# Layer two of a mixture of experts: VectorE transposes dense blocks, TensorE's combination reads with a step, and its products go to four row strips at a time

## The reference: what is computed

```python
grouped = x.reshape(B, g, t, d)                       # 32 groups of t = 32 tokens per sequence
logits = jnp.einsum('bgtd,des->bgtes', grouped, controller) + tie
perm = (logits == jnp.max(logits, axis=-3, keepdims=True)).astype(x.dtype)
dispatched = jnp.einsum('bgtd,bgtes->bgesd', grouped, perm)
inner = jax.nn.relu(jnp.einsum('bgesd,desf->bgesf', dispatched, f1) + bias)
intermediate = jnp.einsum('bgesf,esfd->bgesd', inner, f2)
out = jnp.einsum('bgesd,bgtes->bgtd', intermediate, perm)
```

## Time and profile before

| | before |
|---|---|
| median of 3 runs | 1348.98 us (1346.82 to 1352.07) |
| profiled execution: time | 1353.44 us |
| profiled execution: span from the first to the last instruction | 1351.7 us |
| PE busy | 1203.2 us (89%) |
| DVE busy | 890.0 us (66%) |
| ACT busy | 612.6 us (45%) |
| POOL busy | 583.6 us (43%) |
| mean granted TensorE clock | 0.930 of full |

### The profile page before, as it was taken

The page is one execution under the profiler, slowest core; times in us unless marked ns, Lnnn a source line. Parts: engine busy times, 40 slices in busy tenths (PEclk is TensorE's granted clock), DMA queues, the critical chain, the costliest instruction groups (busy, mean ns, idle before and its releaser), DMA issues. The chain is left out here.

```text
span 1351.7 us, 29427 instructions
## 1 busy us (share of the span) xinstructions
PE 1203.2 (89%) x11456; PEld 830.9 (61%) x11456; DVE 890.0 (66%) x2198; ACT 612.6 (45%) x1143; POOL 583.6 (43%) x799
## 2 busy tenths in 40 slices
PE   5999999976889999999999999993799988898773
PEld 4888888853445555555555555541588877875552
DVE  6555555525666877777777778740578865559994
ACT  3222222201545555556656566552244444366651
POOL 0000000003446767777666666674576734302333
PEclk9999999995999999999999999997799977678986
DMA  6665555549623455555554444203788955453344
GB/s 228 217 217 207 213 210 209 186 156 198 143 68 77 108 126 126 126 126 126 126 125 106 114 113 113 69 17 112 266 260 264 297 168 188 168 190 89 111 128 148
DMA packets 163885, 210.77 MB, mean 156 GB/s; under 512 B 8880, under 2 KB 96560, under 8 KB 162736
## 3 DMA queue, kind: packets, MB, share of 16 engines
q1 hardware_dynamic: 163760, 209.06, 53.3%
HBM read 131.17 MB, written 77.59 MB: 154 GB/s over the span
## 5 line engine op out<-in xcount | busy, mean ns | idle before, releaser
L718 ACT ACTIVATE p_t<-p_bank 128x512 f32<-128x512 f32 (+1 forms) x608 | 310.2, 589 | 222.9 <-PE p_bank L778 217.3
L759 PE MATMUL p_bank<-k_stack,q_stack 96*128 96x512 f32 (+3 forms) x768 | 285.2, 394 | 28.8 <-DMA ident<-in_ident 19.3
L664 DVE CUSTOM_DVE_ANT_0 tried<-p_bank,ban 128x128 bf16<-128x128 f32 (+3 forms) x512 | 236.5, 485 | 86.1 <-PE p_bank L759 86.0
L778 PE MATMUL p_bank<-q_stack,k_stack 97*128 97x512 f32 (+3 forms) x768 | 258.9, 358 | 10.4 <-ACT p_t L718 6.0
L759 PEld LDWEIGHTS p_bank<-k_stack,q_stack 96*128 96x128 f32 x768 | 145.8, 193 | 152.8 <-issue 64.2
L667 DVE TENSOR_REDUCE mx_a<-p_bank 128x1 f32<-128x512 f32 x256 | 175.9, 687 | 62.5 <-PE p_bank L759 61.0
L600 POOL TENSOR_SCALAR_AFFINE_SELECT p_t<-p_t 128x128 f32<-128x128 f32 (+2 forms) x288 | 102.0, 357 | 171.5 <-ACT p_t L718 164.2
L778 PEld LDWEIGHTS p_bank<-q_stack,k_stack 97*128 97x128 f32 x768 | 145.6, 191 | 41.5 <-ACT p_t L718 27.0
L796 PE MATMUL p_bank<-p_t,v_tile 128*32 128x512 f32 (+3 forms) x1536 | 162.9, 497 | 1.6 <-POOL p_t L600 1.2
L611 POOL TENSOR_TENSOR p_sum<-p_sum,p_t 128x512 f32<-128x512 f32 x128 | 159.9, 1281 | 0.5 <-ACT p_t L718 0.5
L584 POOL MEMSET k_stack<- 1x4096 f32 x3 | 10.4, 3506 | 302.3 <-POOLq L128 302.3
(11 more groups left out here) (121 smaller groups left out, 2287.8 us busy)
## 6 DMA issues: line engine op xcount, KB each, us to landing
q_stack<-q_hi SPq DMA_DIRECT2D x64, 256.0 KB, 6.5
k_stack<-k_hi SPq DMA_DIRECT2D x30, 512.0 KB, 9.5
f_sb<-in_f SPq DMA_DIRECT2D x5, 2048.0 KB, 7.9
x_in<-in_x SPq DMA_DIRECT2D x8, 1024.0 KB, 9.1
c_in<-in_ctx_t SPq DMA_DIRECT2D x8, 1024.0 KB, 11.1
k_hi<-k_hi_s SPq DMA_DIRECT2D x8, 1024.0 KB, 4.2
k_lo<-k_lo_s SPq DMA_DIRECT2D x8, 1024.0 KB, 6.4
v_rows<-v_out SPq DMA_DIRECT2D x8, 1024.0 KB, 4.3
```

The source lines that it names most:

```text
L664: dve.tensor_tensor_reduce(tried[:, TRIED[c]:TRIED[c] + w], got, ban0[:] if i == 0 else ban[:, CH - w:CH], 1.0, -3e38, ALU.add, ALU.max, t ...
L718: act.activation(pt[:, k % SLOTS_P, u * m:(u + 1) * m, 0:w], bank[:, SB + n % SR, 0:m * w].rearrange("p (m w) -> p m w", m=m), ACT.Exp, sc ...
L759: pe.matmul(bank[:, to, 0:w], qs[it % SLOTS][0:R, i * P // CH, h, i * P % CH:i * P % CH + P], ks[it % SLOTS][0:R, h, t0:t0 + w], start=Tru ...
L778: mm = pe.matmul(bank[:, SB + n % SR, h % m * w:(h % m + 1) * w], ks[slot][0:R + 1, h, j * P:(j + 1) * P], qs[slot][0:R + 1, sh, h, CH - w ...
```

## The change

`y` is laid out the other way round: `[d, i]` (feature, then expert within the strip) instead of `[i, d]`, and so are the two `y_rows`: `[d, g]` instead of `[g, d]`. VectorE's transpositions then read and write 1024 elements that lie one behind another, where they read with a step of 256 elements (1024 bytes) and wrote with a step of 128 elements (512 bytes). TensorE's combine now reads its 128 moving columns out of `y_rows` with a step of 32 elements (128 bytes), where they were contiguous. ScalarE's keep now takes its elements from PSUM with the bank as the innermost index and writes runs of 4 elements (16 bytes) every 128 bytes, where it read and wrote contiguous runs.

A make now covers two pairs. Which expert sits in which strip and place is permuted (in layer one, and on the host in `f2` and the bias) so that those two pairs use all four row strips `q` with all four column strips `c`: the same 32 products, now with 16 different positions of the array before the first is used again, where a pair used 8. It waits for the banks of both pairs before its first product, and it releases both at its last ones. The makes of unit `u + 2` are split into two pairs after chunk 0 and six after chunk 1.

```diff
-        y = [wide[:, i * IDX * DH:(i + 1) * IDX * DH].rearrange("p (i d) -> p i d", d=DH) for i in range(2)]
-        y_rows = [nc.alloc_sbuf_tensor_at(f"y_rows{i}", [P, GT, P], F32, offset=at)
+        y = [wide[:, i * IDX * DH:(i + 1) * IDX * DH].rearrange("p (d i) -> p d i", i=IDX) for i in range(2)]
+        y_rows = [nc.alloc_sbuf_tensor_at(f"y_rows{i}", [P, P, GT], F32, offset=at)
...
-                    to = y[u % 2].rearrange("p (m q) d -> p q m d", q=4)[:, qp * 2:qp * 2 + 2, mp * 2:mp * 2 + 2]
-                    act.copy(to, bank[:, n % RING * 2:n % RING * 2 + 2].rearrange("p q (m d) -> p q m d", m=2)).then_inc(kept_y, 1)
+                    to = y[u % 2][:, :, pair * 4:pair * 4 + 4].rearrange("p d (m q) -> p d m q", q=2)
+                    act.copy(to, bank[:, n % RING * 2:n % RING * 2 + 2].rearrange("p q (m d) -> p d m q", m=2)).then_inc(kept_y, 1)
...
-                            for pair in (range(RING) if ch == 0 else range(RING, PAIRS)):
+                            for pair in (range(2) if ch == 0 else range(2, PAIRS)):
                                 keep(u + 2, pair)
...
-                        ins = dve.transpose(y_rows[ch][:, :, d:d + ONCE].rearrange("p g d -> p d g"),
-                                            y[u % 2][:, :, ch * P + d:ch * P + d + ONCE].rearrange("p i d -> p d i"))
+                        ins = dve.transpose(y_rows[ch][:, d:d + ONCE],
+                                            y[u % 2][:, ch * P + d:ch * P + d + ONCE])
...
-                                es = e * IDX + n * 4 + q
+                                es = e * IDX + n // 2 * 8 + q // 2 * 4 + n % 2 * 2 + q % 2
...
-                def make(u, pair):
-
-                    b, h, mp, qp = u // HALVES, u % HALVES, pair // 2, pair % 2
-                    n = u * PAIRS + pair
+                def make(u, mp):
+
+                    b, h = u // HALVES, u % HALVES
                     if u == 0:
                         pe.wait_ge(f2_in[mp], 16)
                         pe.wait_ge(active, mp * 2 + 2)
-                    if n >= RING:
-                        pe.wait_ge(kept_y, n - RING + 1)
-                    else:
-                        pe.wait_ge(inner_done, (KD - 1) * NQ + n * 2 + 2)
+                    for n in (u * PAIRS + mp * 2, u * PAIRS + mp * 2 + 1):
+                        if n >= RING:
+                            pe.wait_ge(kept_y, n - RING + 1)
+                        else:
+                            pe.wait_ge(inner_done, (KD - 1) * NQ + n * 2 + 2)
                     for i in range(2):
-                        for q in range(qp * 2, qp * 2 + 2):
-                            part = slice(q * F, (q + 1) * F)
-                            for c in range(4):
+                        for c in range(4):
+                            for q in range(4):
+                                part = slice(q * F, (q + 1) * F)
                                 e = (mp * 2 + i) * 4 + c
+                                n = u * PAIRS + mp * 2 + q // 2
                                 mm = pe.matmul(bank[c * GT:(c + 1) * GT, n % RING * 2 + q % 2, i * DH:(i + 1) * DH],
                                                inner[part, e, b * GT:(b + 1) * GT], f2[e // PIECE][part, e % PIECE, h * DH:(h + 1) * DH],
                                                start=True, stop=True, tile_position=(q * F, c * GT), skip_group_check=True)
-                    mm.then_inc(made, 1)
+                                if i == 1 and c == 3 and q % 2 == 1:
+                                    mm.then_inc(made, 1)
...
-                                               pick[:, i, g * GT:(g + 1) * GT], y_rows[ch][:, (w * UT + n) * GQ + g],
+                                               pick[:, i, g * GT:(g + 1) * GT], y_rows[ch][:, :, (w * UT + n) * GQ + g],
...
-                            for pair in (range(RING) if ch == 0 else range(RING, PAIRS)):
-                                make(u + 2, pair)
+                            for mp in (range(1) if ch == 0 else range(1, PAIRS // 2)):
+                                make(u + 2, mp)
```

More of the change, by code:

```diff
@@ L1481, in _ @@
                 for u in range(2):
-                    for pair in range(PAIRS):
-                        make(u, pair)
+                    for mp in range(PAIRS // 2):
+                        make(u, mp)
                 for u in range(UNITS):
@@ L1541, in layout @@
         "f1": arr(i["L0_ffn_f1"]).reshape(D, NE * F),
-        "bias_col": arr(arr(i["L0_ffn_bias"]).reshape(4, E4 // 4, 4, F).transpose(2, 3, 1, 0)).reshape(P, E4),
-        "f2": arr(arr(i["L0_ffn_f2"]).reshape(4, E4 // 4, 4, F, D).transpose(2, 3, 1, 0, 4)).reshape(P, E4, D),
+        "bias_col": arr(arr(i["L0_ffn_bias"]).reshape(4, 4, 2, 2, 2, F).transpose(2, 4, 5, 1, 3, 0)).reshape(P, E4),
+        "f2": arr(arr(i["L0_ffn_f2"]).reshape(4, 4, 2, 2, 2, F, D).transpose(2, 4, 5, 1, 3, 0, 6)).reshape(P, E4, D),
         "ident": np.eye(P, dtype=np.float32),
```

## The result

The changed kernel takes 1374.34 us (median of 4 runs, 1372.32 to 1378.62), the kernel before, run beside it, 1350.53 us (4 runs, 1346.82 to 1356.97). The ratio is 1.0161, with a 95% interval from 1.0128 to 1.0193: 1.6% slower. The forecast was 1350, its range 1343 to 1361. The time is near the 1370 of the rival that stepped reads make TensorE the limit.

What follows compares the result with a forecast made beforehand. SyncE's queue of stores and loads was taken as the limit, VectorE close beside it. -2.5 (third store) + 1.4 (start) + 2.1 (clock) = +1.0 us on the median 1348.98 gave 1350.0 us, range 1343 to 1361.

Steps and rivals of the forecast that it cites:

- the rival that stepped reads make TensorE the limit: Combine: stepped reads slow TensorE past the queue; at s = 3 a unit is 18.3 us, time 1370; chance 0.10.
- The limit before: SyncE's queue: 32 sums stored, landed and loaded one by one, 3.88 us each, bound the kernel; VectorE offered one each 3.71.
- The rival that VectorE was the limit: Transpositions: VectorE bound the kernel after all, so 30 us less, 1319 us; chance 0.03.
- VectorE's transpositions: Dense transpositions on VectorE: 1238 ns each instead of 1983, 47.7 us less work over 64.
- The combine's reads: TensorE's stepped reads in the combine: taken to cost 0, upper bound a factor 1.6 from VectorE's rows.
- s = 2.3: Combine: the slowdown factor s at which a unit on TensorE reaches the queue's 15.5 us.
- The makes: TensorE's makes: 1.10 us for two pairs, 2.3 us a round with copy and hand-overs; hidden in the loop, not at the start.
- my formula: TensorE's time for one unit of the loop: 6.6 + 3.9 s us, s being the factor on the combines.
- The start and the clock: Before the first store: slower rounds of makes and copies cost +1.4 us, a lower TensorE clock +2.1 us.
- The clock's term: Makes at the start: a less busy TensorE gets a lower clock, +2.1 us, bounds 0 and +6.2.
- The sum: Whole kernel: -2.5 + 1.4 + 2.1 = +1.0 us, likeliest time 1350.0 us.
- The -2.5 us at the third store: Queue's third store: chunks 4.6 us apart instead of 7.4 end its wait for a sum, saving 2.5 us.

Runs made afterwards that it cites:

- e4: The kernel before with each load one store later in the queue: 1342.81 us, ratio 0.9932.
- e7: The changed kernel with each load one store later in the queue: 1371.87 us, ratio 1.0160.
- e3: The kernel before with only the new makes (permuted experts, two pairs a make, split two and six): 1354.81 us, ratio 0.9999.
- e1: The changed kernel with y_rows back at [g, d], so the combine reads contiguously and VectorE writes with a step: 1353.93 us, ratio 1.0018.
- e8: The kernel before with the combine reading at a step of 32 elements, all four column strips reading the same columns: 1366.64 us in one profiled run.
- e11: The changed kernel with the makes of before (one pair a make, three and five pairs): 1353.79 us, ratio 1.0018.
- e2: The kernel before with only the combine's reads changed, to a step of 32 elements: 1371.36 us, ratio 1.0127.
- e9: The kernel before with y as [d, i], y_rows in runs of two elements, and each load one store later: 1321.04 us, ratio 0.9782.
- e6: The kernel before with y_rows in runs of two elements and each load one store later: 1347.29 us, ratio 0.9968.
- e5: The kernel before with y_rows in runs of four elements and each load one store later: 1349.89 us, ratio 0.9992.

## Why the prediction was wrong

**The limit before: right.** I took the queue, not VectorE, for the limit. e4 moved the loads away from their stores and won 0.7%, and e7 shows that the same edit is worth nothing once TensorE is the limit. Its pace I took for steadier than it is: measured alike, from the first store to the last four, it was 4.26 us a sum before, 4.11 in e3 and 3.86 in e1. And I set a unit at 15.5 us, by the pace of the end, where the same rows give 16.9 for the middle. The rival that VectorE was the limit is out: its row fell by 45 us and the time rose.

**VectorE's transpositions: right.** I said 1238 ns each, and they take 1212; 47.7 us less, and it is 44.9. e1 adds that the whole of it hangs on both sides: with one side stepped by 512 bytes next to nothing is won.

**The combine's reads: the step that failed.** "I take 0", with 1.6 as the upper bound from VectorE's rows. A chunk takes 5.53 to 5.59 us in the chain and 5.65 in the timeline of PE, where it took 1.95, so s is 2.8 to 2.9 at full clock, above the point s = 2.3 that I had named as decisive. With it the overlap on which the forecast stood is gone: I had TensorE at 10.5 us a unit, hidden under the queue's 15.5, and it takes 19.2 to 20.2. The bound was borrowed from another engine, and nothing ties the two. A dense transposition takes 1024 elements a partition in 1212 ns, a dense chunk's combine, counted by its records, 64 x 128 = 8192 columns in 1.95 us, five times as many in a ns. That a limit on reads with a step shows sooner on the faster reader is an argument that no run tests; e8 took one explanation from it, the four separate streams. But it should have kept me from taking VectorE's factor for an upper bound. The rule that I quoted, the Trainium skill's "SBUF — State Buffer", section "SBUF: two separate sides" (at least two hits in each 16-byte line), pointed the right way, and the runs agree with it where they can: a step of 8 bytes, two hits a line, took 1.97 to 2.05 us, one of 16 bytes 3.78 to 3.85. That 128 bytes costs still more, 5.5 to 5.7, the rule does not say.

**The makes: right in kind, too small.** I wrote 1.10 us for two pairs and 2.3 for a round; it is 1.47 and 2.65. The old makes take 0.78 and 0.86 us a pair when they stand back to back (three in 2.35 and five in 4.30 us of e11's chain), 1.57 to 1.72 for two, so sixteen positions save 0.1 to 0.3 us in two pairs, not the 0.5 to 0.6 that 1.10 would have been. The copy at 1.02 and the two hand-overs at 0.16 together were close to what I said (1.1 and 0.1). On a unit this is the smaller part: of the 8.7 us above my 10.5, the combines are 7.2 and the makes with their copies 1.5. By my formula a unit is 6.6 + 3.9 x 2.85 = 17.7 us, whereas the trace has 19.24, and four makes of 1.41 to 1.49 instead of 1.1 are 1.4 of the 1.5 between them. But it is the part that tells, since 17.7 is what e11 has, and e11 is not measurably slower than before. In the first two units of the loop one make ran at half the clock besides, 2.37 us instead of 1.49 (at 1244.29 and 1264.46 us); they took 20.2 us.

**The start and the clock: right in kind, too small.** The first store was to move by 1.4 + 2.1 us and moved by 8.0 from the first copy. Seven rounds of 2.65 instead of 2.3 are 2.5 of that. ScalarE then waits 0.98 us for the first sum, which comes after half a stepped combine; I had it wait for nothing. The clock's term is 3.2 us where I had 2.1 (bounds 0 and 6.2): the seven makes of these rounds take 13.5 us, where seven of 1.47 are 10.3, and 2.7 of the difference lies in the last three, at 2.35 to 2.37 us each. Together 1.4 + 2.5 + 1.0 + 3.2 = 8.1. Two stretches of the start of the changed kernel (busy time of PE, PEld, DVE, ACT and POOL, then granted clock, DMA share, GB/s): TensorE was busy for 6.4 of the first 10 us at the full 2.4 GHz, and in the second, with those three makes, it had 1.2.

```profile
1206.00:1216.00 10.00, 6.41 (x256) 3.51 (x255) 0.79 (x1) 6.59 (x8) 0.00 (x0) 1.00 0.02 7
1217.00:1226.50 9.50, 7.13 (x196) 3.35 (x200) 7.34 (x7) 4.69 (x6) 0.00 (x0) 0.50 0.01 3
```

The stepped combines do not follow the clock. In e2 the first one had it at half for at least 3 of its 5.5 us (the combine in the timeline of PE, then the stretch):

```profile
1225.48 5.54 PE L1472 MATMUL p_bank<-y_rows,pick_exp 128*32 128x128 f32 x64 [1.78 <-DVE y_rows L1389]
...
1226.00:1229.00 3.00, 3.00 (x41) 2.16 (x36) 3.00 (x2) 0.53 (x1) 0.00 (x0) 0.51 0.00 0
```

It takes 5.54 us, and e2's others at full clock 5.57 to 5.66, where a dense one went from 1.95 to 3.62. That would fit a combine that waits for its reads; no run shows what it waits for.

**The sum.** I had 1350 as the likeliest; for it to fail two things had to come together, and both did. Either half of the change alone stays at the queue's pace or close to it (the new makes in e1 and e3, the layout in e11: ratios within 0.2% of 1, their intervals within 0.5%); both together are 19.2 to 20.2 us a unit against 16.9. The -2.5 us at the third store had nothing to act on, since the sums came later and not sooner. My rival for this side had the right limit, TensorE, but gave the reads alone as the cause; it put 18.3 us on a unit at s = 3, against 19.2. That its 20 us on the whole came so near to the 19.4 is partly luck: it was 2.8 us in each of seven units over a queue at 15.5, and nothing at the start, where the trace has 13.5 us in the loop, over a queue at 17.1 a unit (119.4 / 7), and 8.0 at the start. I had given it 0.10.

## What stays open

Why the queue takes 4.26 us a sum in the kernel before and 3.86 in e1 is not settled, and so it is open how far the makes of e1 and e3 would stay hidden at the slower pace. That VectorE's stepped transpositions grow while TensorE reads with a step is measured in e2; which resource the two share was not tried. The new makes bring three things at once, the order of the positions, the wait for two pairs of banks and a lower granted clock, and no run parts them. A ring of more than three pairs of banks, which could keep the new makes from alternating with the copies, was not tried.

## What to carry to other kernels

In these runs an access with a step was cheap or dear by its distance in bytes and by the engine that made it: before a layout is turned for one engine, price the same bytes on the engine on the other side, and look for one that serves both (here runs of two elements with the old makes, 2.2% faster, where the fully dense layout with the new makes lost 1.6%; both with the later loads, which alone gave 0.7%). When two limits lie side by side, two changes that cost nothing alone can cost together, so add their parts on each engine for one round of the loop and not over the whole. A make that must find two of the ring's three buffers empty turned the pipeline into an alternation; count copy plus hand-over plus make as one round.

## What was not expected of the hardware

- Combine of one chunk, 64 records of 128 moving fp32 columns, at full clock: contiguous 1.95 us, step of 8 bytes 1.97 to 2.05, 16 bytes 3.78 to 3.85, 128 bytes 5.5 to 5.7. The last is the same with the clock at half for most of it (e2, 5.54) and when all four column strips read the same columns (e8).
- A 32 x 32 block transposition of 1024 fp32 elements a partition on VectorE: 1212 to 1214 ns when the reading side is dense and the writing side is dense or in runs of 8 or 16 bytes; 1.82 us from one to the next when the writing side alone is stepped by 512 bytes (e1), 1.90 and 1.94 when the reading side alone is, with runs of 8 and 16 bytes written (e6, e5), 1.86 when both are.
- Stepped reads of TensorE slow other engines: with a step of 128 bytes, VectorE's stepped transpositions went from 118.8 to 142.5 us in all (e2), 3575 ns each inside a combine and 2012 outside, and GpSimd's additions from 1282 to 1334 ns. VectorE's dense ones did not suffer (1212 in the changed kernel and 1214 in e11, beside 1214 in e9 with its step of 8 bytes). The row of GpSimd's additions in e2:

```profile
L1311 POOL TENSOR_TENSOR x_in<-o_sum,x_in 128x512 f32<-128x512 f32 x32 | 42.7, 1334 | 149.9 <-ACT o_sum L1348 149.9
```

- Products in sixteen positions of the array took 1.41 to 1.49 us for 64 records at full clock, those in eight 1.57 to 1.72 for as many (e11).
